# Second stage of a decoder block: GpSimd's context split earlier in a sequence, LayerNorm and router a step later and in smaller parts

## What is computed

```python
x = x + self_attention(layernorm(x))           # 16 heads, rational softmax, ALiBi, causal
x = x + cross_attention(layernorm(x), ctx)     # 8 heads of 64, context 750 x 384 per sequence, key mask
x = x + moe(layernorm(x)) + bias               # router to 8 experts, top 2, capacity 896, gelu, 512-2048-512

def cross_attention(x, context, mask, W_q, W_k, W_v, W_o, b_o):
    q, k, v = x @ W_q, context @ W_k, context @ W_v
    sim = where(mask, einsum('bihd,bjhd->bhij', q, k) * scale, -FLT_MAX)
    return softmax(sim) @ v @ W_o + b_o
scores = softmax(xf @ w_router); expert_weights, top_experts = top_k(scores, 2)
```

## Time and profile of the kernel before

| | |
|---|---|
| median of 3 runs | 3497.4 us |
| lowest, highest | 3491.75, 3503.05 us |
| the profiled execution | 3495.34 us |
| its span | 3493.6 us |
| TensorE busy | 3107.0 us, 89% |
| VectorE, ScalarE, GpSimd busy | 48%, 40%, 21% |
| mean granted clock of TensorE | 0.943 of full speed |
| second stage, mid sequences | about 79 us each |

### The profile page before, as it was taken

How to read it: one execution, slowest core, us unless ns; L and a number is a source line. 1 busy time by engine, 2 the same in 40 slices (tenths; PEclk the granted TensorE clock), 3 DMA queues, 4 the chain that set the end, 5 groups by cost and what they waited for, 6 DMA issues and landing times. The chain is left out here.

```text
span 3493.6 us, 52659 instructions
## 1 busy us (share of the span) xinstructions
PE 3107.0 (89%) x19340; PEld 2532.3 (72%) x19340; DVE 1690.5 (48%) x3672; ACT 1403.8 (40%) x2345; POOL 726.0 (21%) x564
## 2 busy tenths in 40 slices
PE   5888898958989988999999957999999999999997
PEld 4667777746777767777777735888788878888886
DVE  5888888843555555555555532333233322323232
ACT  5777777624555555555555521111111111111111
POOL 0000000001111121111111113242424242423343
PEclk9899999978999999999999977999999999999999
DMA  2111111122111111111111002131313131313132
GB/s 92 32 37 46 42 42 42 45 68 100 36 41 35 35 45 54 35 35 35 35 41 35 16 27 102 49 97 55 87 53 91 49 91 49 101 53 89 55 85 58
DMA packets 96194, 193.83 MB, mean 55 GB/s; under 512 B 18656, under 2 KB 28640, under 8 KB 94016
## 3 DMA queue, kind: packets, MB, share of 16 engines
q1 hardware_dynamic: 80912, 160.78, 14.9%
q0 software_dynamic: 15152, 31.26, 4.2%
HBM read 144.19 MB, written 47.82 MB: 55 GB/s over the span
## 5 line engine op out<-in xcount | busy, mean ns | idle before, releaser
L1612 DVE CAST f_hh<-f_hf 128x448 fp32r<-128x448 f32 x256 | 116.9, 457 | 891.7 <-ACT f_hf L1636 859.1
L1636 ACT ACTIVATE f_hf<-f_h 128x448 f32<-128x448 f32 x256 | 139.6, 545 | 1015.8 <-PE f_h L1672 987.6
L1688 PE MATMUL f_y<-f_w2h,f_hh 128*128 128x512 f32 x896 | 357.9, 399 | 0.0
L1559 POOL TENSOR_TENSOR f_w1l<-f_raw,f_w1h 128x512 fp32r<-128x512 f32 x130 | 183.4, 1411 | 828.5 <-DVE f_w1h L1594 828.3
L1688 PE MATMUL f_y<-f_w2h,f_hl 128*128 128x512 f32 x896 | 354.1, 395 | 0.0
L1688 PE MATMUL f_y<-f_w2l,f_hh 128*128 128x512 f32 x896 | 352.3, 393 | 0.0
L1247 ACT COPY c_pT<-c_psum 125x672 f32<-125x672 f32 x256 | 184.2, 719 | 311.7 <-PE c_psum L1353 309.9
L1255 ACT ACTIVATE c_s_sb<-c_s_sb,c_nmx 112x750 f32<-112x750 f32 x256 | 236.0, 922 | 161.9 <-DVE c_nmx L1091 159.0
L1672 PE MATMUL f_h<-f_xTh,f_w1h 128*128 128x448 f32 x1024 | 262.2, 378 | 32.5 <-ACT f_hf L1636 16.8
L1353 PEld LDWEIGHTS c_psum<-c_ident,c_s_sb 112*125 112x125 f32 x1536 | 204.1, 198 | 84.4 <-issue 78.1
L1672 PE MATMUL f_h<-f_xTl,f_w1h 128*128 128x448 f32 x1024 | 256.0, 372 | 0.0
(11 more groups left out here) (243 smaller groups left out, 5970.0 us busy)
## 6 DMA issues: line engine op xcount, KB each, us to landing
f_raw<-in_w SPq DMA_DIRECT2D x132, 512.0 KB
c_craw<-in_ctxT SPq DMA_DIRECT2D x16, 1125.0 KB, 5.5
a_x_in<-in_x SPq DMA_DIRECT2D x9, 896.0 KB, 5.6
a_xr<-in_x SPq DMA_DIRECT2D x8, 896.0 KB, 5.9
x_dram<-a_xr SPq DMA_DIRECT2D x8, 896.0 KB, 4.8
q_dram<-a_q SPq DMA_DIRECT2D x32, 224.0 KB, 5.3
c_q<-q_dram SPq DMA_DIRECT2D x16, 448.0 KB, 5.2
c_x<-x_dram SPq DMA_DIRECT2D x16, 448.0 KB, 5.6
```

Of the source, the lines that this page charges most:

```text
L1559: pool.tensor_tensor(w1s[1][:, n % NSLOT].rearrange("p k c -> p (k c)"), raw1[:, g % 2, n % 2, :], w1s[0][:, n % NSLOT].rearrange("p k c - ...
L1612: dve.tensor_copy(hs[0][:, l % 2, c * HC:c * HC + HC], hf[:, c, :]).then_inc(h_hi, 1)
L1636: act.activation(hf[:, c, :], H[:, 0:HC], ACT.Gelu_apprx_tanh).then_inc(free, 1)
L1688: mm = pe.matmul(Y[t][:], hs[a][:, l % 2, 128 * t:128 * t + 128], w2s[b][:, l % NSLOT, :], start=j == 0 and q == 0, stop=j == FB - 1 and q ...
```

## The change

`PLAN` puts K(0, 0) into step 6 in place of XT(0), XT(0) into the last slot of step 7 and XT(1) into that of step 8, and the router's RT into step 10 instead of 9. With that the two XT units share one bank. ScalarE reads XT(0) and XT(1) out as it does K and V: at the beginning of the next step, ahead of the row copy. Its three casts of the context go to the front of step 4, behind the last V unit's copy and ahead of the row copy. The reciprocal square root goes from step 4 to 5, the routing's exponential from 10 to 11.

VectorE adds the second output block in step 5 instead of 4, and takes each block's statistics right behind its addition; LayerNorm goes from step 5 to 6, the routing's first half from 10 to 11. GpSimd's xo waits for both blocks of xn. SyncE stores xn first, then xo. A semaphore is renamed.

```diff
-                4: ([], [OUT(1)], []), 5: ([], [PV(0)], []), 6: ([], [XT(0)], []), 7: ([K(0, 0)], [K(0, 1)], [XT(1)]),
-                8: ([], [K(1, 0)], []), 9: ([], [PV(1)], [RT]), 10: ([], [V(0, 0)], []), 11: ([K(1, 1)], [K(2, 0)], []),
+                4: ([], [OUT(1)], []), 5: ([], [PV(0)], []), 6: ([], [K(0, 0)], []), 7: ([], [K(0, 1)], [XT(0)]),
+                8: ([], [K(1, 0)], [XT(1)]), 9: ([], [PV(1)], []), 10: ([], [V(0, 0)], [RT]), 11: ([K(1, 1)], [K(2, 0)], []),
...
         def projections(kind, s, slots):
-            return [u for u in units(kind, s, slots) if u[0] in ("K", "V")]
+            return [u for u in units(kind, s, slots) if u[0] in ("K", "V", "XT")]
...
             def store(i):
 
+                wait_apart(sp, xn_made, i * 2)
+                sp.dma_start(flat(one(xn_v, i - 1), "r j c"), xn[:]).then_inc(xn_stored, 16)
                 wait_apart(sp, xo_made, i)
                 sp.dma_start(flat(one(out_v, i - 1), "r j c"), xo[:]).then_inc(out_stored, 16)
-                wait_apart(sp, xn_made, i * 2)
-                sp.dma_start(flat(one(xn_v, i - 1), "r j c"), xn[:]).then_inc(xn_stored, 16)
...
-                if s == 8:
+                if s == 9:
+                    wait_apart(pool, xn_made, i * 2)
                     pool.wait_ge(out_stored, i * 16 - 16)
-                    pool.wait_ge(gen_free[BANK[kind, OUT(1)]], uses_before(i, kind, OUT(1)) + 1)
                     pool.tensor_tensor(xo[:], x1[:], bi[:, None, :].broadcast_to([R, 2, C]), ALU.add).then_inc(xo_made, 1)
...
-                if j == 0:
-                    return
-                for j in range(2):
-                    wait_apart(dve, gen_free[BANK[kind, OUT(j)]], uses_before(i, kind, OUT(j)) + 1)
-                    ins = dve.bn_stats(stats[:, j, :], x1[:, j, :])
-                ins.then_inc(stats_made, 1)
-                wait_apart(dve, stats_made, i)
-                for j in range(2):
-                    dve.bn_aggr(mv[:, j, :], stats[:, j, :]).then_inc(mv_made, 1)
+                wait_apart(dve, gen_free[b], uses_before(i, kind, OUT(j)) + 1)
+                dve.bn_stats(stats[:, j, :], x1[:, j, :]).then_inc(stats_made[j], 1)
+                wait_apart(dve, stats_made[j], i)
+                dve.bn_aggr(mv[:, j, :], stats[:, j, :]).then_inc(mv_made, 1)
...
-                if s in (3, 4):
-                    residual(i, kind, s - 3)
-                elif s == 5:
+                if s in (3, 5):
+                    residual(i, kind, s // 4)
+                elif s == 6:
                     layernorm(i)
-                elif s == 10:
+                elif s == 11:
                     routing(i, kind, 0)
...
             def tail(i, kind, s):
-                if s == 4:
+                if s == 5:
                     act.wait_ge(mv_made, i * 2)
                     act.activation(rstd[:], mv[:, :, 1], ACT.Abs_reciprocal_sqrt, bias=eps[:]).then_inc(root_made, 1)
-                elif s in (7, 8):
-                    unit = XT(s - 7)
-                    act.wait_ge(gen_full, number(ORDER, i, kind, unit) + 1)
-                    act.copy(xnT[:, s - 7, :], bank(kind, unit)[:, 0:KC * R]).then_inc(gen_free[BANK[kind, unit]], 1)
-                elif s == 10:
+                elif kind == "end" and s in (7, 8):
+                    evacuate(i, kind, XT(s - 7))
+                elif s == 11:
...
+                    if s == 4 and kind != "last":
+
+                        act.wait_ge(gen_full, number(ORDER, i, kind, V(1, 2)) + 1)
+                        hi_of_context(i + 1)
                     for unit in projections(kind, s, (0,)):
                         evacuate(i, kind, unit)
                     if s > 0:
...
                         exponential(*step(i, s + 2))
-                    if s == 4 and kind != "last":
-
-                        act.wait_ge(gen_full, number(ORDER, i, kind, V(1, 2)) + 1)
-                        hi_of_context(i + 1)
...
                 elif what == "RT":
-                    for j in range(2):
-                        made(i, kind, XT(j))
+                    made(i, kind, XT(1))
+                    if BANK[kind, XT(0)] != BANK[kind, XT(1)]:
+                        made(i, kind, XT(0))
```

More of the change, by code:

```diff
@@ L868, in unit_places @@
             what, m, a = unit
+            if what == "XT":
+                return xnT[:, m, :], bank(kind, unit)[:, 0:KC * R]
             if what == "K":
@@ L886, in cross_attention @@
         trash_set, trash_ready, trash_stored = sem("trash_set"), sem("trash_ready"), sem("trash_stored")
-        c_loaded, q_madeaded, m_loaded, x_loaded = sem("c_loaded"), sem("q_madeaded"), sem("m_loaded"), sem("x_loaded")
+        c_loaded, q_loaded, m_loaded, x_loaded = sem("c_loaded"), sem("q_loaded"), sem("m_loaded"), sem("x_loaded")
         xn_stored, out_stored = sem("xn_stored"), sem("out_stored")
@@ L896, in cross_attention @@
         x1b_made, xo_made = sem("x1b_made"), sem("xo_made")
-        stats_made, mv_made, root_made, rstd_made, xn_made = (sem(n) for n in ("stats_made", "mv_made", "root_made", "rstd_made", "xn_made"))
+        stats_made = [sem("stats_made0"), sem("stats_made1")]
+        mv_made, root_made, rstd_made, xn_made = (sem(n) for n in ("mv_made", "root_made", "rstd_made", "xn_made"))
         newton = sem("newton")
@@ L944, in load_queries @@
             def load_queries(i):
-                sp.dma_start(q2[:], flat(one(q2_dram, i), "p k t")).then_inc(q_madeaded, 16)
+                sp.dma_start(q2[:], flat(one(q2_dram, i), "p k t")).then_inc(q_loaded, 16)
             load_context(0)
@@ L1236, in copy_queries @@
             def copy_queries(i, g):
-                act.wait_ge(q_madeaded, i * 16 + 16)
+                act.wait_ge(q_loaded, i * 16 + 16)
                 act.copy(q[:, 2 * g:2 * g + 2], q2[:, 2 * g:2 * g + 2]).then_inc(q_made, 1)
```

## The result

The changed kernel takes 3394.1 us in the median of 4 runs (3388.5 to 3401.3), the kernel before 3495.2 on the same chip: a ratio of 0.971, 95% interval 0.9696 to 0.9724. That is 101 us faster, where 115 was forecast (3380), inside the range of 3345 to 3425. The profiled execution took 3391.7 us around a span of 3390.0.

What follows compares the result with a forecast made beforehand. TensorE's own order was taken to bound the second stage, with 11.5 us per sequence hanging on LayerNorm. 7.9 us in each of 14 sequences (111) plus 4 elsewhere took 3495.3 to 3380 us; own range 3364 to 3396, whole 3345 to 3425.

Steps and rivals of the forecast that it cites:

- Part 1: Context split earlier: ScalarE's casts ahead of step 4's row copy cost nothing; a normalising op is charged 0.6 to 1.1 us.
- S8: Start of the scores that TensorE issues in step 8; S with another number means the same for that step.
- Part 2: Stretch up to S8: with VectorE's statistics moved, TensorE no longer waits for the row maximum; gain 2.0 us per sequence.
- Part 3: S8 to S10: VectorE's op, held by GpSimd's addition, is late next; 14.94 us becomes 9.1, gain 5.8 per sequence.
- S10: Start of the scores that TensorE issues in step 10, forecast at S8 + 9.1 us behind a 2.4 us wait.
- rival B: VectorE's normalising op starts before GpSimd's addition: S10 at S8 + 7.4 us, 9.7 gained per sequence, 3353 us; chance 0.18.
- A: Rival: TensorE's clock falls in the gap left ahead of S10; 5.3 us gained per sequence, 3417 us; chance 0.22.
- Part 5: S12 onward: the router's work moves in, loss 1.15 us, and the later routing costs another 0.5 per sequence.
- S16: Start of step 14's successor scores, in step 16; forecast unharmed though its maxima come about 1.4 us later.
- S12: Start of the scores that TensorE issues in step 12; S10 to S12 was forecast to gain 1.75 us.
- Rival D: The change doesn't do what it says: K(0,0) still waits or routing costs its bound; half the gain, 3438 us; chance 0.08.
- C: Rival, slower: TensorE's low clock lasts through S12 and beyond; 3549 us with 12 us of such work; chance 0.04.

Runs made afterwards that it cites:

- b1: The kernel before with one edit: ScalarE's three casts of the context in front of step 4's row copy; 3440.4 us, ratio 0.9851.
- e3: The changed kernel with ScalarE's three casts of the context back behind the exponential of step 4; 3350.5 us, 0.9592 of the kernel before.
- e6: The changed kernel with GpSimd's addition for xo also waiting for VectorE's normalising op of row block 8; 3344.7 us, 0.9573 of the kernel before.
- e7: e6 with the router's matmul back in step 9 and the routing's first half in step 10; 3358.3 us, 0.9618 of the kernel before.
- v1: The kernel before with only the change's casts, residual additions, statistics, LayerNorm and xo, in the old order of units; 3487.1 us, ratio 0.9988.
- b2: The kernel before with GpSimd's addition for xo waiting until xn is done, and xn stored first; 3493.3 us, ratio 1.0003.
- e4: The changed kernel with the router's matmul back in step 9 and the routing's first half in step 10; 3395.7 us, 0.9717 of the kernel before.
- e2: The changed kernel with GpSimd's addition for xo split into two instructions, one per row block; 3356.9 us, 0.9604 of the kernel before.
- e1: The changed kernel with GpSimd's addition for xo on its old trigger, the second output block's addition; 3353.1 us, 0.9602 of the kernel before.
- u1: The kernel before with only the change's new order of units, early copies of XT and router's move; 3431.1 us, ratio 0.9829.
- e9: The same kernel as e6, run again on another chip; 3353.9 us, 0.9606 of the kernel before.

## Why the prediction was right, and where not

Part 1 is right in what it says (the casts fill ScalarE's idle time, K(0,0) has its operand in time, S8 isn't held; the normalising op charged with 0.6 to 1.1 us of blocking takes 0.70 instead of 0.61), and b1 shows that the casts alone gain 52 us on the kernel before. Not foreseen was that in the changed kernel they cost some 40 us against the late place (e3), because they bring LayerNorm's end, and with it the start of GpSimd's addition, to the wrong side of VectorE's op.

Part 2 is right to 0.04 us, by the table.

Part 3's mechanism is right in each link: S10 at S8 + 9.05 where +9.1 was worked out, a TENSOR_SCALAR of 2.37 us (2.4), a wait of 2.53 (2.4). e6, which changes only the order of the two starts, brings +7.30, beside rival B's value of 7.4. The step that was off is its left side: 14.94 us is the one sequence that I read. The mean of 14 is 14.29: the K projection behind XT(0)'s copy starts at S8 + 11.1 in all of them, but how much of what follows runs at the low clock differs. So the gain is 5.24, not 5.8, 8 us in the sum.
```profile
996.70 0.68 PE L1321 MATMUL c_psum<-c_cTh,c_wkl 128*128 128x376 f32 x3
...
1466.69 0.57 PE L1396 MATMUL c_psum<-c_ident,c_xn 112*128 112x112 f32 x4 [2.27 <-DVE c_xn L1126]
1467.04 0.76 PE L1321 MATMUL c_psum<-c_cTh,c_wkh 128*128 128x376 f32 x3
1467.63 0.97 PE L1321 MATMUL c_psum<-c_cTl,c_wkh 128*128 128x376 f32 x3
1468.40 1.15 PE L1321 MATMUL c_psum<-c_cTh,c_wkl 128*128 128x376 f32 x3
```

So the trace on which the forecast rests already spoke for A.

Part 5 is right in kind and close in size: +1.01 for +1.15, S16 unharmed, +0.36 for +0.5. As a whole it looked like a loss of 1.65 us against 1.67 moved out of S10 to S12, and e7 agrees that the balance is near nothing.

Two terms were in none of the parts: 0.24 us in S2 to S4, which comes and goes in one and the same kernel, and some 6 us of the 104 between the two spans, which the third stage has in its own time without a change to it. These 6 us are luck: without them and the 1 us of the first stage the profile shows 97 us of gain where 115 was forecast. The forecast's own lower end is a slip too: its stated terms give 3369, not 3364.

Rival D found nothing for it. Nor did C: the low clock lasts 3.4 us in 11 sequences and 6.8 in two (S10 to S12 is 10.27 there), not longer than before. That it can last far longer is shown by v1, with 13.8 us.

## What to carry to other kernels

Where GpSimd and VectorE share a stretch, ask of each GpSimd instruction which VectorE op stands next behind its trigger. A trigger that looks natural (LayerNorm is done, so the residual may go out) put a 2.4 us block on the critical chain, and one wait more, for the op that must be first, gained some 40 us (0.971 of the kernel before became 0.957 and 0.961). Moving an op elsewhere so that it is not blocked is no gain if the next link of the same chain takes the block over (b2), and a step that ends earlier can be a loss when something else starts on it (e3 against the changed kernel). When a term of the sum is the length of a stretch, take its mean over the repetitions, not the one that was read; and what one repetition doesn't show, as here the clock that fell, look for in the others.

## What the runs showed of the hardware that I had not expected

- The clock of TensorE falls behind a single wait of 2.5 us in otherwise dense work, in 13 of 14 sequences (in 12 of 14 in e4, with the same wait), and behind waits of 1.44 us (e2) and 0.76 us (e1, e6) in none. Between them it is neither always nor never: behind the wait of 1.98 us ahead of S8 it fell in 4 of 14 sequences in u1 and in b2 each, and in u1 in 7 of 14 about where waits of 1.35 and 0.84 us stand close together.
- ScalarE's first row copy behind the jump of its loop comes later in some sequences than in others, and in some profiles in none. In the sequence shown of the changed kernel and in e1, whose streams are the same there:

```profile
1026.27 0.72 ACT L1245 COPY c_pT<-c_psum 125x672 f32<-125x672 f32 x1 [1.42 <-PE c_psum L1349]
```

```profile
1021.43 0.72 ACT L1245 COPY c_pT<-c_psum 125x672 f32<-125x672 f32 x1 [0.39 <-PE c_psum L1349]
```

It starts 1.97 us behind the transposes it reads (at 1024.30) in the one and 0.95 (at 1020.48) in the other, and TensorE loses 0.57 us in each such sequence (S2 to S4 9.83 or 9.27): in 10 of 14 in the changed kernel, in none in e1, e2, e3 and e6. e6 and e9, one kernel, differ in this step, 9.26 against 9.67 on average, and in no other by more than 0.02. Its cause stays open; no run tells it.
- GpSimd's ops are held as well as they hold: the addition for xo takes 2.76 us instead of 2.37 where VectorE was first (e3).
